# Writing the output over the input image, spreading chunk decays by one selection product, and a reordered head with fourteen extra products

## The chip, the cores and the metric

The kernel runs on one core of one Trainium2 chip. The metric is the device time of the whole program in microseconds (us), the median over several runs.

## The reference, cut to what matters

The input is a batch of 4 images, 128 channels by 32 x 32 pixels in float32, so each image is a 128 x 1024 matrix. Two layers follow each other. The first is an attention block: group norm, q, k, v, a softmax over 1024 x 1024 scores, projection, and the residual. The second is a Mamba-2 block:

```python
u = layernorm(tokens)                       # per token, 128 channels
z, xBC, dt = split(u @ in_w.T)
dt = softplus(dt + dt_bias)                 # 4 heads
x, B, C = split(silu(depthwise_conv4(xBC)))
state = state * exp(dt * A) + (dt * x) outer B   # per token and head
y = state . C + D * x
y = rmsnorm(y * silu(z)) ; out = y @ out_w.T
out = x_in + out * sigmoid(se2(relu(se1(mean(out)))))
```

The recurrence is computed in chunks of 128 tokens. With la = dt * A the log of one token's decay, three things are needed per chunk: the matrix L of decays between all pairs of tokens in it, the decay from the chunk's start to each token (`decay_in`, the exponential of the running sum of la), and the decay over the whole chunk (`chunk_decay`, the exponential of the sum of la over all 128 tokens).

## The kernel before, in words

Each image (a, b, c, d) goes through about 315 named steps. The string `ORDER` (line 59) lists all 1267 steps of the four images in one sequence, and each engine walks that list and issues only the steps that are its own (the loops `for kind, n, b, _ in STEPS`). The order on every engine's queue is therefore the order of that string, written out by hand or by a planner, and every dependence is a semaphore wait in front of an instruction. An instruction that waits holds back everything behind it on its engine. The string also gives, after an `@`, which of the three PSUM banks of the second layer a step fills. The wait for the previous user of that bank to be read is put in by `fill` (line 348 on) from the table `bank_read`.

A half is 512 tokens, four chunks; n = 0 or 1 is the half, and h is one of four heads. `R` = 16 is chunks times heads of a half. Per image and half the steps around the change are:

- `sp0` to `sp8` (DVE, `softplus`): the softplus and la, 16 numbers per token and half. `sp8` writes `la`.
- `dA` (ACT, line 596): exp(la). `dA_rows` (DVE, `rows_split`, lines 671 and 673): the 16 columns in two parts, a rounded one and the rest, 32 columns. `DAT` (PE, line 1051): their transpose, and beside it in the same bank a product of `ones` with la, which is the sum over the chunk. `dA_T` (DVE, line 857): the transposed rows times a mask, `dA_head`, 128 x 512 in the rounded type float32r. `L` (PE, four of them): one product of a row selector with `dA_head`. `l` (DVE, line 872): a scan over each gives L.
- `cd` (ACT, line 603): exp of the chunk sums, `chunk_decay`.
- `Dec` (PE): 16 products in float32, one per chunk and head, each of 32 output partitions by 128 columns, la against the triangular matrix `upto`; every product is two instructions. `decay` (ACT, line 610): exp of the result, `decay_in`. `yo` (DVE, line 901) multiplies by it.
- `y` (DVE, line 907) writes the tile `y`, `g` (POOL, line 484) gates it, `sq`, `Ss`, `ms`, `y_pow`, `y_rows`, `YrT`, `y_T`, `YrB`, `y_b` form the norm, `Out` and `o` (line 926) the output product, `SeA`, `hdn`, `SeB`, `tha`, `att` the squeeze, `XR` (line 1156) a transpose of the residual, and `fin` (line 936) the final sum.

`fin` writes over the tile `y` (`o_img, fin = y, y`), and the SP queue sends it to memory (line 394). So `y` of the next image first waits for that transfer:

```python
wait(dve, yo_dx_ready, b, n + 1)
wait(dve, out_sent[n], b - 1, 16)
```

The head of the program: POOL writes constants, DVE builds the selection masks (`head_of`, `chunk_of`, `head_mask`, lines 657 to 666), then `gn_stats0`, `gn_dev0`, `gn_ve0`, `gn_aff0` (DVE), `gn_mm10` and `gn_mm20` (PE) and `gn_pow0` (POOL) form the group norm of image a. `h_hi` and `h` (ACT, lines 516 and 510) and `h_lo` (DVE, line 776) write the normalised image in two parts, `Q`, `q_hi` (line 522), `q_lo` (line 780) form the query, `S` the scores (three products of 128 x 512 each), `max` (line 784), `exp` (line 533), `T` and `pT` the transposed probabilities, and `PV` the product with the values. `gn_stats1` is the statistics of images b to d: six instructions on DVE. `kq_mm`, `vp_mm`, `win_mm` and `kq_ev`, `vp_ev`, `win_s`, `win_ev` prepare weights. Tiles of PSUM are called `scores`, `turn` (V and T), `attn_out` (PV) and `mamba` (the second layer).

## Time and profile before

| | |
|---|---|
| median of 3 runs | 328.7 us (328.65 to 328.84) |
| the profiled execution | 328.64 us |
| its span, first to last instruction | 326.9 us |
| busy: PE (matmul) / weight load / DVE | 284.5 / 232.1 / 261.0 us |
| busy: ACT / POOL | 187.3 / 81.9 us |
| mean granted TensorE clock | 0.974 of full |

The profiled execution took 1.7 us more than its span. Busy time of an engine does not say that it sets the time: the stretches of the program differ, and the rows below give them separately. A matmul's duration includes the way through the array, so products in a row overlap, and what one costs is the distance from start to start.

### The profile page before, as it was taken

To read this page: it belongs to the slowest core of one execution; us is meant where nothing else is said; L and a number is where in the kernel's file an instruction comes from. 1 tells how busy PE (TensorE), PEld (TensorE's weight loads), DVE (VectorE), ACT (ScalarE), POOL (GpSimd) and SP (SyncE) were. 2 spreads that over 40 slices of the span, in tenths; PEclk is the share of its full clock that TensorE was granted. 3 is DMA by queue.
4 is the path that set the end of the run, shared out by engine and by line. 5 is a ranking of instruction groups with operands and counts; after the bars stand their busy time and mean duration, and the time that the engine had idled before them with its cause. 6 is when DMAs were issued, how large, how long until landed. Compare 5 with 4: busy or idle time off the path is not lost.

```text
span 326.9 us, 6452 instructions
## 1 busy us (share of the span) xinstructions
PE 284.5 (87%) x2206; PEld 232.1 (71%) x2206; DVE 261.0 (80%) x586; ACT 187.3 (57%) x347; POOL 81.9 (25%) x99
## 2 busy tenths in 40 slices
PE   0598999999999999899999999999999988756663
PEld 0477897897879778676787877887987765445542
DVE  4674475997798978969989998988999988996523
ACT  1324577978786855666587656566574835641011
POOL 6000100001011025541502522162023176107340
PEclk9999999999999999999999999999999999996777
DMA  7900000000000000000000000000000010000101
GB/s 216 369 6 1 2 0 3 0 2 0 2 1 3 0 2 2 0 3 1 2 1 9 25 34 1 2 0 3 3 0 2 2 64 1 3 0 2 64 0 66
DMA packets 3791, 7.34 MB, mean 22 GB/s; under 512 B 656, under 2 KB 1584, under 8 KB 3760
## 3 DMA queue, kind: packets, MB, share of 16 engines
q1 hardware_dynamic: 3216, 6.72, 5.7%
q8 instruction: 19, 0.31, 0.4%
q10 hardware_dynamic: 544, 0.21, 0.2%
q14 instruction: 12, 0.10, 0.1%
HBM read 4.83 MB, written 2.10 MB: 21 GB/s over the span
## 4 chain that ended last, share of the span: by engine, by line
PE 57%; DVE 26%; issue 7%; ACT 4%; POOL 2%; DMA 2%; DVEq 1%; ACTq 0%; POOLq 0%
PE mamba L947 20%; PE attn_out L947 12%; PE scores L947 12%; PE turn L1015 6%; DVE L L872 4%; DVE pre L822 3%; DVE neg_max L784 3%; PE turn L947 2%; DMA out<-y 2%; DVE gn_raw L707 1%; PE mamba L1073 1%; DVE scanned L892 1%; DVE L L884 1%; DVE y L936 1%; DVE y L907 1%
## 5 line engine op out<-in xcount | busy, mean ns | idle before, releaser
L947 PE MATMUL attn_out<-values,pT 128*128 128x129 f32 x512 | 66.8, 276 | 0.3 <-DVE res L793 0.2
L947 PEld LDWEIGHTS attn_out<-values,pT 128*128 128x128 f32 x512 | 62.9, 191 | 4.2 <-issue 2.8
L533 ACT ACTIVATE probs<-scores,neg_max 128x512 f32<-128x512 f32 x64 | 42.8, 684 | 25.8 <-DVE neg_max L784 20.4
L784 DVE TENSOR_REDUCE neg_max<-scores 128x1 f32<-128x1024 f32 x32 | 39.0, 1218 | 15.5 <-PE scores L947 15.1
L539 ACT ACTIVATE pT<-turn 128x512 f32<-128x512 f32 x64 | 37.4, 594 | 14.4 <-PE turn L1015 8.9
L872 DVE TENSOR_TENSOR_SCAN L<-mamba,ident 128x512 f32<-128x512 f32 x32 | 38.2, 1212 | 2.3 <-PE mamba L947 2.1
L1015 PE MATMUL turn<-ident,probs 128*128 128x128 f32 x256 | 37.8, 273 | 0.0
L822 DVE SCALAR_TENSOR_TENSOR pre<-raw,vec,pre 128x512 f32<-128x512 f32 x48 | 37.5, 789 | 0.2
L947 PE MATMUL scores<-h_hi,q_hi 128*128 128x512 f32 x64 | 31.4, 491 | 3.4 <-ACT probs L533 2.5
L1015 PEld LDWEIGHTS turn<-ident,probs 128*128 128x128 f32 x256 | 30.2, 141 | 5.8 <-issue 3.3
L445 POOL TENSOR_TENSOR ln_rstd<-ln_var,neg_half 128x4 f32<-128x4 f32 x8 | 8.5, 1066 | 81.1 <-DVE ln_var L804 81.1
L463 POOL TENSOR_TENSOR xend<-xdt,to_end 128x512 f32<-128x512 f32 x8 | 9.8, 1228 | 74.3 <-DVE xdt L865 39.0
L947 PE MATMUL scores<-h_hi,q_lo 128*128 128x512 f32 x64 | 25.8, 404 | 0.0
L947 PE MATMUL mamba<-u,winC 128*128 128x512 f32 x48 | 24.9, 604 | 0.9 <-DVE L L872 0.4
L947 PE MATMUL scores<-h_lo,q_hi 128*128 128x512 f32 x64 | 25.6, 400 | 0.0
L884 DVE TENSOR_TENSOR L<-L,mamba 128x512 f32<-128x512 f32 x32 | 21.3, 678 | 1.0 <-PE mamba L947 1.0
L456 POOL TENSOR_TENSOR gate<-gate,zv 128x512 f32<-128x512 f32 x16 | 20.5, 1286 | 3.6 <-ACT gate L584 3.4
L947 PEld LDWEIGHTS scores<-h_hi,q_hi 128*128 128x128 f32 x64 | 12.3, 192 | 11.1 <-issue 7.6
L947 PE MATMUL mamba<-dA_head,pick_chunk 128*128 128x512 f32 x32 | 14.3, 468 | 2.4 <-ACT BT L616 0.6
L623 ACT ACTIVATE stateT<-scanned 128x512 f32<-128x512 f32 x8 | 9.2, 1145 | 12.1 <-DVE scanned L892 12.1
L484 POOL TENSOR_TENSOR xs<-y,gate 128x512 f32<-128x512 f32 x8 | 11.0, 1380 | 13.8 <-DVE y L907 13.8
L947 PEld LDWEIGHTS scores<-h_hi,q_lo 128*128 128x128 f32 x64 | 12.3, 192 | 2.9
(189 smaller groups left out, 572.1 us busy)
## 6 DMA issues: line engine op xcount, KB each, us to landing
res<-in_x_tok SPq DMA_DIRECT2D x4, 512.0 KB, 8.1
out<-y SPq DMA_DIRECT2D x8, 256.0 KB, 2.0
x_all<-in_x SPq DMA_DIRECT2D x3, 512.0 KB, 8.0
x_all<-in_x SPq DMA_DIRECT2D x2, 256.0 KB, 3.2
winT<-in_in_wT SPq DMA_DIRECT2D x1, 194.0 KB, 6.4
wqkv<-in_qkv_w ACTq DMA_DIRECT2D x1, 192.0 KB, 3.6
wpT<-in_proj_wT SPq DMA_DIRECT2D x1, 64.0 KB, 3.6
ob_row<-in_proj_b SPq DMA_DIRECT2D x1, 64.0 KB, 5.5
```

The costliest lines, as they stand in the source:

```text
L456: pool.tensor_tensor(gate[:, half], gate[:, half], zv[:, half], ALU.add if part else ALU.mult).then_inc(gate_ready.sem, 1)
L463: pool.tensor_tensor(xend[:, rows, :], xdt[:, rows, :], to_end[:, rows].unsqueeze(2).broadcast_to([P, R, HEADDIM]), ALU.mult).then_inc(xen ...
L484: pool.tensor_tensor(y2[:, half], y[:, half], gate[:, half], ALU.mult).then_inc(y2_ready.sem, 1)
L533: act.activation(probs[:, i % 2, half_of(h)], scores[:, half_of(h)], ACT.Exp, bias=neg_max[:, i:i + 1]).then_inc(exp_done.sem, 1)
L539: act.activation(pT[:, i % 2, QUAD * h:QUAD * (h + 1), :], bank[:, :].rearrange("p (a b) -> p a b", a=QUAD), ACT.Copy).then_inc(pT_ready.s ...
L623: act.activation(stateT[:, n, :, :], scanned[:, n, :, :].rearrange("s e c -> s c e"), ACT.Copy).then_inc(stc_ready.sem, 1)
L784: V.tensor_reduce(neg_max[:, n:n + 1], scores[:, :], AX.X, ALU.max, negate=True).then_inc(max_ready.sem, 1)
L822: V.scalar_tensor_tensor(pre[:, k, half_of(n)], raw[:, k, n * HALF + j:(n + 1) * HALF + j], vec[:, at + j:at + j + 1], pre[:, k, half_of(n ...
L872: V.tensor_tensor_scan(L[:, HEADS * n:HEADS * (n + 1), :].rearrange("p a b -> p (a b)"), bank[:, :], ident4[:, :, :].rearrange("p a b -> p ...
L884: V.tensor_tensor(M[:, HEADS * n:HEADS * (n + 1), :], L[:, HEADS * n:HEADS * (n + 1), :], bank[:, tile(c)].unsqueeze(1).broadcast_to([P, H ...
L947: return T.matmul(o, w, v, start=start, stop=stop)
L1015: last = T.transpose(bank[:, tile(c)], probs[:, i % 2, tile(QUAD * h + c)], ident[:, :])
```

## The change

It does four things.

1. `fin` writes into `x_all`, the input image of the same batch, and the SP queue sends from there. `y` waits for `fin` of the image before in place of its transfer.
2. A new step `Cum` (PE) takes a bank of its own and computes from la two sums of 16 columns: the running sum (`upto`) and the chunk's sum (`ones`, until now in `DAT`). A new step `dec` (ACT) takes exp of the running sum. `cd` reads the chunk's sum from that bank. `dA_rows` splits exp(la) and exp(running sum) together, 32 columns, and `DAT` transposes both. The mask keeps the new rows by chunk, and `Dec` is one product of a head selector with `dA_head`, which now comes after `dA_T`. `decay` is a copy in place of an exponential.
3. The masks are built otherwise: four reductions in place of two, `head_sel` of 128 columns and one more copy, and the big mask is a sum of two broadcast tiles in place of a copy.
4. `ORDER` is another order throughout, the head included, with two steps `warm3` and `warm11` on PE: 3 and 11 products of `ident` with itself, 128 x 128 in float32, into `scores`, without a wait.

```diff
 ORDER = """
-gn_stats0 kq_mm gn_mm10 vp_mm gn_dev0 gn_mm20 vp_ev gn_ve0 gn_pow0 gn_aff0 kq_ev h_hi0a win_s h_hi1a win_mm h0a h1a
-h_lo0a xob0a h_lo1a gn_stats1 Q0a V0a@1 q_hi0a q_lo0a gn_mm11 v0a xob1a Q1a S0a q_hi1a alog q_lo1a xob0b S1a V1a@1
-max0a gn_dev1 exp0a v1a S2a exp1a T0a@1 gn_mm21 pT0a S3a T1a@1 max1a PV0a pT1a PV1a exp2a T2a@0 inv0a res0a S4a pT2a
-exp3a S5a T3a@0 max2a PV2a pT3a win_ev PV3a exp4a exp5a T4a@0 S6a gn_ve1 inv1a pT4a gn_pow1 res1a stats0a S7a T5a@0
-max3a PV4a pT5a xob1b PV5a exp6a exp7a T6a@0 inv2a stats1a S8a res2a pT6a xob0c S9a gn_aff1 stats2a T7a@1 max4a PV6a
...
-stc1d XR0c@1 fin0c m5d gate3d Yo1d@1 m6d Y0d@2 yo1d m7d XR1c@1 yo_dx1d y0d Y1d@0 fin1c g0d y1d g1d sq0d Ss0d@0 sq1d
-ms0d Ss1d@2 y_pow0d Out0d@0 ms1d y_rows0d y_pow1d YrT0d@2 y_T0d YrB0d@2 y_rows1d YrT1d@1 y_b0d y_T1d YrB1d@1 o0d
-Out1d@2 y_b1d XR0d@0 o1d SeA0d@2 XR1d@1 hdn0d SeB0d@2 tha0d att0d fin0d fin1d
+gn_stats0 warm3 vp_mm gn_mm10 vp_ev kq_mm gn_dev0 xob0a gn_mm20 kq_ev gn_ve0 gn_pow0 gn_aff0 xob1a h0a wo_s h_hi0a
+win_s h_hi1a h_lo0a h1a warm11 Q0a h_lo1a q_hi0a Q1a q_lo0a q_hi1a S0a q_lo1a gn_stats1 S1a win_mm V0a@1 V1a@0 max0a
+gn_mm11 xob0b exp0a xob1b exp1a S2a v0a gn_dev1 S3a v1a T0a@0 max1a T1a@1 pT0a PV0a exp2a alog exp3a S4a pT1a S5a PV1a
+max2a T2a@0 inv0a T3a@1 xob0c exp4a gn_mm21 exp5a S6a gn_ve1 pT2a xob1c gn_pow1 S7a pT3a res0a T4a@0 max3a PV2a pT4a
+PV3a exp6a exp7a S8a inv1a res1a gn_aff1 T5a@0 stats0a S9a xob0d pT5a h0b T6a@1 stats1a max4a PV4a PV5a win_ev exp8a
+exp9a S10a pT6a xob1d S11a inv2a res2a T7a@0 stats2a max5a T8a@1 pT7a PV6a h1b PV7a exp10a exp11a S12a inv3a pT8a
...
+Yo0d@0 xend1d m1d dx0d U1d@1 yo0d m2d gate2d SeB0c@0 m3d tha0c G1d@0 att0c st1d dx1d yo_dx0d m4d stc1d XR0c@1 gate3d
+m5d fin0c Yo1d@2 m6d Y0d@1 yo1d m7d XR1c@2 yo_dx1d y0d Y1d@0 fin1c g0d y1d g1d sq0d Ss0d@2 sq1d ms0d Ss1d@0 y_pow0d
+y_rows0d ms1d YrT0d@1 y_pow1d Out0d@0 y_T0d YrB0d@2 y_rows1d YrT1d@1 y_b0d y_T1d o0d YrB1d@2 Out1d@1 y_b1d o1d SeA0d@2
+hdn0d SeB0d@2 XR0d@1 tha0d XR1d@0 att0d fin0d fin1d
 """.split()
...
 PREPARE = ("gn_stats", "gn_mm1", "gn_dev", "gn_mm2", "gn_ve", "gn_pow", "gn_aff", "kq_mm", "kq_ev", "vp_mm", "vp_ev",
-           "win_s", "wo_s", "win_mm", "win_ev", "alog")
+           "win_s", "wo_s", "win_mm", "win_ev", "alog", "warm")
 ATTENTION = {"xob", "h", "h_hi", "h_lo", "Q", "q_hi", "q_lo", "V", "v", "S", "max", "exp", "T", "pT", "PV", "inv", "res"}
...
         pick_row = sb("pick_row", [P, QUAD], F32R)
-        head_of = sb("head_of", [P, HEADS])
-        chunk_of = sb("chunk_of", [P, QUAD])
+        head_sel = sb("head_sel", [P, HEADS, HEADDIM], F32R)
+        row_head, row_chunk = sb("row_head", [P, 2, HEADS]), sb("row_chunk", [P, 2, QUAD])
         head_mask = sb("head_mask", [P, HEADS, P])
...
         la = sb("la", [P, 2, R])
-        dA = sb("dA", [P, 2, R])
+        dA = sb("dA", [P, 2, 2 * R])
         dA_rows = sb("dA_rows", [P, 2, P])
...
         y = sb("y", [P, TOKENS])
-        o_img, fin = y, y
+        o_img = y
         y2 = xs
...
         filled = {kind: signal(f"{kind}_filled", n) for kind, n in (
-            ("V", 2), ("T", 16), ("UT", 2), ("InX", 2), ("InBC", 2), ("InZ", 2), ("Dt", 2), ("DAT", 2), ("Dec", 2),
+            ("V", 2), ("T", 16), ("UT", 2), ("InX", 2), ("InBC", 2), ("InZ", 2), ("Dt", 2), ("Cum", 2), ("DAT", 2), ("Dec", 2),
             ("L", 8), ("XsT", 2), ("BT", 2), ("G", 2), ("U", 2), ("Yo", 2), ("Y", 2), ("Ss", 2), ("YrT", 2),
...
         sp_step = signal("sp_step", 2 * SP_STEPS)
+        dec_ready = signal("dec_ready", 2)
         dA_ready, dA_rows_step, dA_T_ready = signal("dA_ready", 2), signal("dA_rows_step", 4), signal("dA_T_ready", 2)
...
                      "InBC": [(raw_ready["bc"], 1)], "InZ": [(zt_ready, 1), (zv_ready, 1)], "Dt": [(dtx_step, 1)],
-                     "DAT": [(dA_T_ready, 1), (cd_ready, 1)], "Dec": [(decay_ready, 1)], "L": [(l_ready, 1)],
+                     "Cum": [(dec_ready, 1), (cd_ready, 1)], "DAT": [(dA_T_ready, 1)], "Dec": [(decay_ready, 1)], "L": [(l_ready, 1)],
                      "XsT": [(xdt_ready, 1)], "BT": [(BT_ready, 1)], "G": [(M_ready, 4)], "U": [(st_ready, 1)],
...
                     wait(sp, fin_ready, b, n + 1)
-                    sp.dma_start(out_d[b][:, half_of(n)], fin[:, half_of(n)]).then_inc(out_sent[n].sem, 16)
+                    sp.dma_start(out_d[b][:, half_of(n)], x_all[:, b * TOKENS + n * HALF:b * TOKENS + (n + 1) * HALF]
+                                 ).then_inc(out_sent[n].sem, 16)
             for n in range(2):
...
                     wait(act, sp_step, b, SP_STEPS * (n + 1))
-                    act.activation(dA[:, n, :], la[:, n, :], ACT.Exp, scale=1.0 / A_SCALE).then_inc(dA_ready.sem, 1)
+                    wait(act, dA_rows_step, b - 1, 2 * n + 2)
+                    act.activation(dA[:, n, 0:R], la[:, n, :], ACT.Exp, scale=1.0 / A_SCALE).then_inc(dA_ready.sem, 1)
+                elif kind == "dec":
+                    wait(act, dA_rows_step, b - 1, 2 * n + 2)
+                    bank = take(act, b, "Cum", n)
+                    act.activation(dA[:, n, R:2 * R], bank[:, 0:R], ACT.Exp, scale=1.0 / A_SCALE).then_inc(dec_ready.sem, 1)
                 elif kind == "cd":
                     wait(act, st_ready, b - 1, n + 1)
-                    wait(act, dA_T_ready, b, n + 1)
-                    bank = take(act, b, "DAT", n)
+                    bank = take(act, b, "Cum", n)
                     chunks = slice(1, QUAD) if n == 0 else slice(0, QUAD - 1)
                     act.activation(chunk_decay[:, n, :, :, 1:QUAD],
-                                   bank[:, P:P + R].rearrange("s (c h) -> s h c", h=HEADS)[:, :, chunks]
+                                   bank[:, R:2 * R].rearrange("s (c h) -> s h c", h=HEADS)[:, :, chunks]
                                    .unsqueeze(2).broadcast_to([P, HEADS, HEADDIM, QUAD - 1]),
...
                     bank = take(act, b, "Dec", n)
-                    act.activation(decay_in[:, half], bank[:, :], ACT.Exp, scale=1.0 / A_SCALE
-                                   ).then_inc(decay_ready.sem, 1)
+                    act.activation(decay_in[:, half], bank[:, :], ACT.Copy).then_inc(decay_ready.sem, 1)
                 elif kind == "bt":
...
             V.tensor_scalar(center[:, :], ident[:, :], 1.0 / P, None, ALU.subtract)
-            V.tensor_reduce(head_of[:, :], ident[:, 0:2 * R].rearrange("r (q h) -> r h q", h=HEADS), AX.X, ALU.add)
-            V.tensor_reduce(chunk_of[:, :],
-                            ident[:, 0:2 * R].rearrange("r (s c h) -> r c s h", s=2, c=QUAD), AX.XY, ALU.add)
-            V.memset(head_mask[:, :, 0:1], 0.0)
+            rows = ident[:, 0:4 * R].rearrange("r (s k c h) -> r k s c h", s=2, k=2, c=QUAD)
+            for k in range(2):
+                V.tensor_reduce(row_head[:, k, :], rows[:, k].rearrange("r s c h -> r h s c"), AX.XY, ALU.add)
+                V.tensor_reduce(row_chunk[:, k, :], rows[:, k].rearrange("r s c h -> r c s h"), AX.XY, ALU.add)
             step_done(V.tensor_tensor(pick_row[:, :], ident[:, 0:QUAD], ident[:, QUAD:2 * QUAD], ALU.add))
-            V.tensor_copy(pick_chunk[:, :], chunk_of[:, :])
-            step_done(V.tensor_copy(head_mask[:, :, 1:P], head_of[:, :].unsqueeze(2).broadcast_to([P, HEADS, P - 1])))
+            V.tensor_copy(pick_chunk[:, :], row_chunk[:, 0, :])
+            V.tensor_copy(head_sel[:, :, :], row_head[:, 1, :].unsqueeze(2).broadcast_to([P, HEADS, HEADDIM]))
+            V.tensor_copy(head_mask[:, :, 0], row_chunk[:, 1, :])
+            step_done(V.tensor_tensor(head_mask[:, :, 1:P], row_head[:, 0, :].unsqueeze(2).broadcast_to([P, HEADS, P - 1]),
+                                      row_chunk[:, 1, :].unsqueeze(2).broadcast_to([P, HEADS, P - 1]), ALU.add))
             def rows_split(rows, value, signal, b, n):
...
                     if k == SP_STEPS - 1:
-                        wait(dve, filled["Dec"], b - 1, n + 1)
-                        wait(dve, filled["DAT"], b - 1, n + 1)
+                        wait(dve, filled["Cum"], b - 1, n + 1)
+                        wait(dve, dA_ready, b - 1, n + 1)
                     softplus(b, n, k).then_inc(sp_step.sem, 1)
...
                     wait(dve, dA_ready, b, n + 1)
+                    wait(dve, dec_ready, b, n + 1)
                     wait(dve, filled["DAT"], b - 1, n + 1)
...
                     wait(dve, filled["L"], b - 1, QUAD * (n + 1))
+                    wait(dve, filled["Dec"], b - 1, n + 1)
                     bank = take(dve, b, "DAT", n)
...
                     wait(dve, yo_dx_ready, b, n + 1)
-                    wait(dve, out_sent[n], b - 1, 16)
+                    wait(dve, fin_ready, b - 1, n + 1)
                     bank = take(dve, b, "Y", n)
...
                     bank = take(dve, b, "XR", n)
-                    V.scalar_tensor_tensor(fin[:, half], o_img[:, half], att[:, :], bank[:, :], ALU.mult, ALU.add
-                                           ).then_inc(fin_ready.sem, 1)
+                    V.scalar_tensor_tensor(x_all[:, b * TOKENS + n * HALF:b * TOKENS + (n + 1) * HALF], o_img[:, half],
+                                           att[:, :], bank[:, :], ALU.mult, ALU.add).then_inc(fin_ready.sem, 1)
             for kind, n, b, _ in STEPS:
...
                 b0, b1 = (0, 1) if n == 0 else (1, BATCH)
-                if kind == "gn_mm1":
+                if kind == "warm":
+                    for _ in range(n):
+                        mm(scores[:, 0:P], ident[:, :], ident[:, :])
+                elif kind == "gn_mm1":
                     pe.wait_ge(gn_stats_done.sem, n + 1)
...
                     bank, done = fill(pe, b, "DAT", n)
-                    T.transpose(bank[:, 0:P], dA_rows[:, n, :], ident[:, :])
-                    mm(bank[:, P:P + R], ones[:, :], la[:, n, :]).then_inc(done, 1)
+                    T.transpose(bank[:, 0:P], dA_rows[:, n, :], ident[:, :]).then_inc(done, 1)
+                elif kind == "Cum":
+                    wait(pe, sp_step, b, SP_STEPS * (n + 1))
+                    bank, done = fill(pe, b, "Cum", n)
+                    mm(bank[:, 0:R], upto[:, :], la[:, n, :])
+                    mm(bank[:, R:2 * R], ones[:, :], la[:, n, :]).then_inc(done, 1)
                 elif kind == "Dec":
-                    wait(pe, sp_step, b, SP_STEPS * (n + 1))
+                    wait(pe, dA_T_ready, b, n + 1)
                     bank, done = fill(pe, b, "Dec", n)
-                    for c in range(QUAD):
-                        for h in range(HEADS):
-                            r = HEADS * c + h
-                            last = mm(bank[h * HEADDIM:(h + 1) * HEADDIM, tile(c)],
-                                      la[:, n, r:r + 1].broadcast_to([P, HEADDIM]), upto[:, :])
-                    last.then_inc(done, 1)
+                    mm(bank[:, :], head_sel[:, :, :].rearrange("r h d -> r (h d)"),
+                       dA_head[:, n, :, :].rearrange("r h i -> r (h i)")).then_inc(done, 1)
                 elif kind == "L":
...
```

## Rows read from the trace of the kernel before

**Rows 1.** The page: busy time of each engine.
```profile
PE 284.5 (87%) x2206; PEld 232.1 (71%) x2206; DVE 261.0 (80%) x586; ACT 187.3 (57%) x347; POOL 81.9 (25%) x99
```

**Rows 2.** The chain of waits, shares of the span by engine.
```profile
PE 57%; DVE 26%; issue 7%; ACT 4%; POOL 2%; DMA 2%; DVEq 1%; ACTq 0%; POOLq 0%
```

**Rows 3.** Busy time by stretch: five engines, then granted clock and DMA.
```profile
53.00:250.00 197.00, 190.85 (x1513) 159.18 (x1512) 175.76 (x384) 135.50 (x254) 46.90 (x43) 1.00 0.01 4
250.00:293.00 43.00, 34.99 (x338) 25.02 (x337) 39.43 (x84) 24.34 (x47) 15.12 (x13) 1.00 0.04 13
...
293.00:303.00 10.00, 5.74 (x27) 4.74 (x26) 7.34 (x13) 1.16 (x1) 6.15 (x7) 0.66 0.01 2
303.00:313.00 10.00, 6.33 (x84) 5.03 (x84) 4.45 (x8) 1.23 (x2) 4.31 (x4) 0.83 0.14 52
313.00:327.00 14.00, 7.67 (x36) 4.93 (x36) 4.22 (x14) 1.74 (x5) 1.54 (x2) 0.76 0.11 39
```

**Rows 4.** The head in order of time: start, duration, engine, line (idle before, releaser).
```profile
7.31 0.42 DVE L666 COPY head_mask<-head_of 128x508 f32<-128x508 f32 x1
...
13.03 1.52 ACT L516 ACTIVATE h_hi<-x_all,gn_bias,gn_scale 128x512 fp32r<-128x512 f32 x2 [8.27 <-DVE gn_bias L728]
...
17.10 3.65 DVE L707 BATCH_NORM_STATS2 gn_raw<-x_all 128x6 f32<-128x512 f32 x6
...
17.19 0.77 PE L947 MATMUL scores<-h_hi,key_query_hi 128*128 128x512 f32 x1
...
18.62 1.91 PE L947 MATMUL turn<-value_proj,h 128*128 128x128 f32 x8
18.86 0.69 ACT L522 ACTIVATE q_hi<-scores,col 128x512 fp32r<-128x512 f32 x1 [2.90 <-PE scores L947]
...
21.05 0.70 DVE L780 SCALAR_TENSOR_TENSOR q_lo<-scores,col,q_hi 128x512 fp32r<-128x512 f32 x1
...
26.58 1.23 DVE L784 TENSOR_REDUCE neg_max<-scores 128x1 f32<-128x1024 f32 x1 [1.20 <-PE scores L947]
...
28.98 0.40 PE L947 MATMUL scores<-h_lo,q_hi 128*128 128x512 f32 x1
...
29.21 0.40 PE L947 MATMUL scores<-h_hi,q_lo 128*128 128x512 f32 x1
```

**Rows 5.** PE in order of time around one `Dec`.
```profile
70.56 1.08 PE L947 MATMUL mamba<-upto,la 128*32 128x128 f32 x32
71.57 0.50 PE L947 MATMUL mamba<-dA_head,pick_chunk 128*128 128x512 f32 x1
71.91 1.05 PE L947 MATMUL turn<-value_proj,h 128*128 128x128 f32 x8
```

**Rows 6.** Groups by line and shape: busy us, mean ns of one, idle before.
```profile
L947 PE MATMUL mamba<-la,ones 128*128 128x16 f32 x16 | 2.3, 222 | 0.0
...
L596 ACT ACTIVATE dA<-la 128x16 f32<-128x16 f32 x8 | 1.7, 212 | 3.7 <-DVE la L699 3.7
```

**Rows 7.** Groups of DVE from 262 to 311 us.
```profile
L884 DVE TENSOR_TENSOR L<-L,mamba 128x512 f32<-128x512 f32 x8 | 5.3, 677 | 0.0
...
L907 DVE TENSOR_TENSOR y<-mamba,th 128x512 f32<-128x512 f32 x4 | 2.8, 692 | 3.6 <-DMA out<-y 3.0 <-PE mamba L947 0.6
```

**Rows 8.** The end in order of time.
```profile
307.12 1.08 PE L947 MATMUL mamba<-L,xdt 128*32 128x128 f32 x32
307.38 0.74 DVE L936 SCALAR_TENSOR_TENSOR y<-y,att,mamba 128x512 f32<-128x512 f32 x1
...
310.27 0.69 DVE L907 TENSOR_TENSOR y<-mamba,th 128x512 f32<-128x512 f32 x1 [2.15 <-DMA out<-y]
...
311.10 1.13 PE L947 MATMUL mamba<-ones,sq 128*128 128x128 f32 x8 [2.90 <-DVE y L907]
...
314.69 1.91 PE L947 MATMUL mamba<-xs,woutT 128*128 128x512 f32 x2
...
316.39 0.42 PE L1131 MATMUL mamba<-ident,y_rows 128*128 128x128 f32 x1
```

121 lines of the change are left out of this document (60 added, 61 removed).

## The prediction

> **What bounds the kernel now.** I read the busy times first [rows 1]: PE 284.5 us of the span of 326.9 us, DVE 261.0. An average over the span decides nothing, so next the chain of waits [rows 2]: PE holds 57% of it and DVE 26%, which says two engines take turns. The busy time by stretch says where [rows 3]. From 53 to 250 us PE is busy 190.85 of 197 us, 97%, and DVE 89%: PE's queue sets the pace, and what it no longer has to do can come off. From 250 to 293 us the attention of the last image runs out, and DVE is the fuller one, 39.43 of 43. From 293 us on neither is full (PE 21 us of 34 and at a granted clock of 0.66 to 0.83, DVE 16): there the program waits along one chain, and only a shorter chain counts. The head is also a chain, up to the first `max0a` at 26.58 us [rows 4]. So there are four stretches and four sums.
>
> **The head.** Added: DVE builds the masks before `gn_stats0`, and the big mask copy ends at 7.73 us just ahead of it [rows 4]. Two reductions more, two more copies, and a sum of 508 columns where a copy of 0.42 us stood. A sum of 512 columns of the same kind takes 0.68 us [rows 7], so that is 0.26, and small steps follow each other at 0.1 to 0.2 us each: 0.8 in all. On DVE `vp_ev`, `xob0a` and `kq_ev` now stand ahead of `gn_ve0`, while `vp_mm` and `kq_mm` surround `gn_mm10` on PE. Part of them fills waits, and I charge 0.6. Thus `h` starts at 13.03 + 1.4 = 14.4 in place of 13.03.
> Removed: PE had `win_mm` between `h_hi` and `Q0a`, which began at 17.19, 4.2 after the start of `h_hi`. In the new order `h0a`, `h_hi0a` (0.76 each) and `h_lo0a` (0.7) lead to `Q0a` at 16.7. The larger part is `gn_stats1`: 3.65 us on DVE from 17.10 [rows 4], ahead of `q_lo0a`, whose input was ready at 19.55 and which started at 21.05; and `Q1a` stood on PE behind `gn_mm11`, which needs these statistics. Now `gn_stats1` comes after `q_lo1a`, and `win_mm` and both `V` after `S1a`. From `Q0a` at 16.7 through `q_hi`, `q_lo` (0.7 to 0.75 each) and `S0a` I get `q_lo1a` done at 20.5, and `S1a` at 21.4. Next late is DVE itself: `gn_stats1` and three aggregates, 3.9 us, stand before `max0a`, so 24.4. `win_mm` and `V` lie beside it on PE. That is 26.58 - 24.4 = 2.2 us gained.
> The fourteen products: eight products of 128 x 128 last 1.91 us in the head and 1.05 us at 71.91 [rows 4, 5], the three of `S` start 0.23 us apart once the pace is up (28.98, 29.21) [rows 4]. So PE ran at its half level, 1.2 GHz, in the head, and the rise came late. `warm11` issues after `gn_mm20` at about 12 us, where PE would wait, and lasts at the half pace 22 instructions of 1.91 / 8 = 0.24 us or less, some 5 us: up to `Q0a` at 16.7, hence nearly free. If PE is at 2.4 GHz by then, the 2.2 holds. If not, `Q0a` to `S1a` cost some 0.7 more on the chain and `win_mm` and `V` do not fit behind DVE. The price of the warm products themselves is 0 to 0.5 us; I take 0.
> The Trainium skill ("TensorE: Matmul & The Clock Gate", Part 1) says that the array is throttled by default, that activity releases it and idleness takes it back, with a phase that differs from run to run. By that rule the gain could differ between executions, and the pause of PE after `V1a` could take it back; the sum of this head would then be 0 in place of -2.2. The sum goes by the rows' pace.
>
> **`Dec`, `Cum`, `dec`.** A `Dec` begins at 70.56 and the next product at 71.57: 1.01 us of PE, eight times [rows 5]. The new one is one product like the three of `S`, 0.23 us apart [rows 4]. The chunk's product moves from `DAT` to `Cum`; a second like it is new, two instructions of 222 ns that overlap [rows 6]: 0.2 us. So 1.01 - 0.23 - 0.2 = 0.58 per half, 4.6 in all. Seven of the eight stand before the last `PV15d`, where PE's queue sets the pace: 4.1. How much comes off: all of it if nothing else is late, none if waits take it back. The three banks now serve 24 `Cum`, `DAT`, `Dec` in place of 16, and each turn must be read first. I take two thirds, -2.7, because PE had 3% idle and DVE 11% there [rows 3].
> The Trainium skill ("Perfetto Trace Analysis", Identifying the Most-Contended Engine) holds that matmul occupancy is a poor measure and the share of weight loads a better one. Here weight loads fill 159.18 of 197 us, 81%, in that stretch [rows 3]. By that rule PE has a fifth of slack and the saving would come out nearer a third, -1.4.
> ACT gets eight `dec` of 0.21 us, like `dA` [rows 6], 1.7 us beside 69% occupancy: nothing. `decay` costs the same as a copy. DVE's `dA_rows` grow from 16 to 32 columns: 0 to 0.03 us each for 16 instructions, and I take 0.2 into the head's round number.
> The wait: `dA_rows` (DVE) now also waits for `Cum` (0.3 with its way through the array) and `dec` (0.21 and two signals), about 0.7 us more from la to the rows. Behind it on DVE stand `max` and `inv` of attention. The order puts one to eight other DVE steps between `sp8` and `dA_rows` in each of the eight halves, never less than a scan or two products with the chunk matrix, 1.2 us [rows 7], so I cost it at nothing; without cover it is 0.7 x 8 = 5.6 us.
>
> **After the attention.** DVE is the fuller engine here. The new order leaves more behind `PV15d`: `m6c`, `m7c`, `dA_rows0d`, `dA_T0d` for one tap of a convolution, `conv_bc3d`. `m` takes 0.68 [rows 7], `dA_T` and the tap are 512-column steps too and cancel, and the two small ones of `dA_rows` take some 0.2 us: 2 x 0.68 + 0.2 = +1.6 us. The waits of `y` on transfers were 3.0 us over three times [rows 7], of which 2.15 at 310.27 [rows 8] and 0.85 in this stretch: -0.85. The last `Dec` left the chain ahead of `xdt0d`: about -0.6. Sum +0.2.
>
> **The end.** `fin1c` ends at 308.12 and `Y1d` at 308.20; `y1d` starts at 310.27 only because of the transfer [rows 8]. Now it starts at 308.25: -2.0. What is late next is `Y1d`, in the same place. The first `Ss` waited until 311.10 because it shared a bank with `Y1d` [rows 8]; it has another bank now and starts at about 309.6. In the old order `Out0d`, 1.91 us at the half clock, ran from 314.69 ahead of the first transpose of the norm at 316.39 [rows 8], whose rows were ready a microsecond earlier. The new order has it behind. -1.0 for both. Sum -3.0; with the clock lower or higher in between, -2 to -3.5.
>
> **Sum.** -2.2 - 2.7 + 0.2 - 3.0 = -7.7 against the profiled execution's 328.64 us (span 326.9 and 1.7 around it), 0.06 under the median of 328.7. That gives 321.0 us. A measurement of this kernel can tell 0.2% or 0.66 us from no change.
>
> **The rivals.** (1) *The middle gives back.* Everything between 53 and 290 us stands in another order, and the three banks turn over 8 times more. For it: DVE at 89 to 92% leaves little room. Against: the sums of work per image are otherwise the same. Then the Dec saving is 0 and the new order costs 2: -2.2 + 2 + 0.2 - 3.0 = -3.0, 325.7 us. (2) *The head's clock stays low*, or the statistics before `max0a` come no sooner: the head gives 0, -5.5, 323.2 us. (3) *The decay chain becomes the bound, slower.* `dA_rows` blocks DVE while PE and ACT, each in order, come to `Cum` and `dec` behind attention products and exponentials. Ahead of `Cum` on PE can stand as much as a `V`, 1.05 us [rows 5], ahead of `dec` on ACT a 512-column step like `q_hi`, 0.69 us [rows 4]. At 1.0 us per half the 8 halves give back the whole 7.7; at 1.2 us it is 9.6, giving 330.6 us. It decides from 1.0 us of mean stall. Against: the 1.2 us and more of DVE work between `sp8` and `dA_rows`. (4) *The order is better than its parts*: the new interleaving also takes half of the 6 us that PE is idle from 53 to 250 us [rows 3]: -7.7 - 3.1 = -10.8, 317.8 us.
>
> **Numbers.** Forecast 0.50, rival 1 0.20, rival 2 0.12, rival 3 0.08, rival 4 0.10. The range from 317.0 to 327.0 holds rival 4, the forecast, rivals 2 and 1. It leaves out rival 3 and the ends. Faster by over 0.2%: 0.90, with a little of rival 1 going to the same, 0.03; slower 0.07.
>
> **What would show it.** `max0a` near 24.4 us, and the products of `Q0a` 0.23 us apart and not 0.43. No `mamba<-upto,la` group of 256 instructions, PE busy some 5 us less apart from the warm ones. No wait of line 907 on a transfer. From `y1d` to the end 1 us shorter. The last `PV15d` about 5 us earlier. The forecast is wrong if DVE waits for ACT before `dA_rows` by 1 us or more, if PE's idle time from 53 to 250 us grows from 6 us by as much as was saved, or if the stretch after `PV15d` is longer by more than 2 us.

## The result and the profile after

| | before | after |
|---|---|---|
| median, 4 runs of each side by side | 328.8 us (328.65 to 329.86) | 317.05 us (316.62 to 317.42) |
| the profiled execution | 328.64 us | 316.84 us |
| its span | 326.9 us | 315.0 us |
| mean granted TensorE clock | 0.974 | 0.984 |

The ratio is 0.9636, with a 95% interval of 0.9611 to 0.9661. The change takes 11.7 us off where 7.7 was forecast. The median lies 0.05 us above the lower end of the range, 317.0; the ratio times 328.8 us gives 316.8, just below it. The page's busy times and the granted clock in 40 slices, to hold against [rows 1] and [rows 2]:

```profile
PE 280.2 (89%) x2002; PEld 228.1 (72%) x2002; DVE 260.7 (83%) x589; ACT 187.1 (59%) x355; POOL 79.7 (25%) x99
PEclk9999999999999999999999999999999999969997
```

DVE and ACT have the work they had (260.7 us against 261.0, 187.1 against 187.3). The page's shares of the chain add up to 17% only, since here it could be followed back over the last part alone, so they can't be read beside [rows 2]. The windows can. After, by stretch, columns as in [rows 3]:

```profile
53.00:240.00 187.00, 180.14 (x1296) 149.00 (x1294) 166.61 (x363) 128.97 (x247) 42.93 (x41) 1.00 0.01 4
...
281.00:291.00 10.00, 8.00 (x40) 5.38 (x41) 9.23 (x13) 4.64 (x9) 1.34 (x2) 0.82 0.01 2
291.00:301.00 10.00, 7.39 (x102) 5.89 (x100) 9.54 (x16) 1.67 (x3) 8.30 (x10) 1.00 0.09 35
```

In the middle PE is as full as before (96% against 97%). The change of character is late: in the two stretches of 10 us DVE is now busy 9.23 and 9.54 us, where [rows 3] had 7.34 and 4.45, and the granted clock is 0.82 and 1.00 in place of 0.66 and 0.83.

**Four marks.** Four instructions can be found in every trace: the first `max0a`, the last product of the last `PV15d` on PE, the last `inv` on DVE (`inv7d`), and the last `y` (`y1d`). They cut the span in five stretches:

| stretch | before | after | difference | forecast by the same cut |
|---|---|---|---|---|
| start to `max0a` | 26.58 | 24.22 | -2.4 | -2.2 |
| `max0a` to the last `PV15d` (263.0; 257.7) | 236.4 | 233.5 | -2.9 | -2.7 |
| `PV15d` to `inv7d` (263.45; 259.57) | 0.45 | 1.87 | +1.4 | +1.6 |
| `inv7d` to `y1d` (310.27; 300.04) | 46.82 | 40.47 | -6.35 | -0.85 - 0.6 - 2.0 = -3.45 |
| `y1d` to the end | 16.63 | 14.96 | -1.7 | -1.0 |
| sum | 326.9 | 315.0 | -11.9 | -7.7 |

The prediction's "After the attention" began where PE ends `PV15d`. Most of the DVE steps that its +1.6 compares (`m7c`, `dA_T0d`, `conv_bc3d`) run ahead of `inv7d`, so it stands in the third line, and the waits and the last `Dec` in the fourth. That the third line agrees says little: `y0c` (0.69 us) stood behind `inv7d` before and stands ahead of it now, and the forecast did not have that. The cut that does not depend on the place of `inv7d` is from the last `PV15d` to `y1d`, before and after:

```profile
263.00:310.27 47.27, 33.89 (x303) 23.83 (x301) 37.90 (x77) 18.04 (x34) 21.11 (x19) 0.89 0.06 23
257.70:300.04 42.34, 32.97 (x252) 22.31 (x251) 38.32 (x80) 19.18 (x37) 18.78 (x18) 0.92 0.04 14
```

It is 4.9 us shorter where 1.85 was forecast (+1.6 - 3.45), and this is where the sum failed. DVE's work in it grew by 0.4 us, 37.9 to 38.3, and its idle time fell from 9.4 to 4.0. The windows of the kernel before, `inv7d` to `y1d` and then to the end:

```profile
263.50:310.30 46.80, 33.39 (x296) 23.45 (x288) 37.42 (x77) 18.04 (x34) 20.63 (x19) 0.89 0.06 20
310.30:326.90 16.60, 8.80 (x44) 5.90 (x44) 5.04 (x16) 2.34 (x5) 3.30 (x3) 0.80 0.09 33
```

The same two of the changed kernel:

```profile
259.60:300.00 40.40, 31.69 (x244) 21.32 (x243) 36.41 (x76) 18.07 (x35) 18.34 (x18) 0.92 0.04 14
300.00:315.00 15.00, 7.42 (x44) 5.20 (x44) 5.14 (x16) 2.97 (x6) 4.02 (x4) 0.89 0.14 52
```

DVE does 37.4 us of work before and 36.4 after, and its idle time is 46.8 - 37.4 = 9.4 us before and 40.4 - 36.4 = 4.0 after: the idle time that went lies all in here, and it is 5.4 of the 6.35 us. The view of its waits names them. Before, in this stretch (total us, times, longest):

```profile
DVE y L907 <- DMA out<-y: 3.0, 3, 2.2
DVE scanned L892 <- PE mamba L947: 1.8, 1, 1.8
DVE th L901 <- PE mamba L947: 0.9, 1, 0.9
DVE xdt L865 <- PE mamba L1073: 0.8, 2, 0.5
DVE dtx L808 <- PE mamba L947: 0.7, 1, 0.7
DVE y L907 <- PE mamba L947: 0.6, 1, 0.6
```

After:

```profile
DVE y_T L933 <- PE mamba L1149: 1.1, 2, 0.7
DVE xs L850 <- PE mamba L960: 0.6, 1, 0.6
DVE L L884 <- PE mamba L960: 0.5, 2, 0.3
DVE th L913 <- PE mamba L960: 0.4, 1, 0.4
```

The transfers' 3.0 us are gone. Of the five waits of 0.6 to 1.8 us for PE, 4.8 in all, three are gone and two are down to 0.4 and 0.2, while others have come, the largest 1.1. The net of these is 9.4 - 4.0 - 3.0 = 2.4 us. The forecast had counted the transfers and 0.6 for the last `Dec`. The last 1.0 of the 6.35 is work (37.4 to 36.4) that now stands ahead of `inv7d`, `y0c` among it.

### The profile page after: what moved, and what is told of

Its sections match the earlier page's. It is cut to its first block and busy times, and to the rows that moved or that the text cites. A ratio compares the mean times of both kernels' runs of the same rounds, so it can differ in the third digit from the quotient of the medians.

```text
span 315.0 us, 6079 instructions
## 1 busy us (share of the span) xinstructions
PE 280.2 (89%) x2002; PEld 228.1 (72%) x2002; DVE 260.7 (83%) x589; ACT 187.1 (59%) x355; POOL 79.7 (25%) x99
## 5 line engine op out<-in xcount | busy, mean ns | idle before, releaser
L542 ACT ACTIVATE pT<-turn 128x512 f32<-128x512 f32 x64 | 37.9, 595 | 19.5 <-PE turn L1032 15.3
L833 DVE SCALAR_TENSOR_TENSOR pre<-raw,vec,pre 128x512 f32<-128x512 f32 x48 | 36.0, 761 | 0.2
L960 PE MATMUL scores<-h_hi,q_hi 128*128 128x512 f32 x64 | 29.1, 454 | 3.4 <-ACT probs L536 2.6
L459 POOL TENSOR_TENSOR gate<-gate,zv 128x512 f32<-128x512 f32 x16 | 20.5, 1279 | 3.1 <-ACT zv L592 2.9
L960 PE MATMUL mamba<-dA_head,pick_chunk 128*128 128x512 f32 x32 | 15.6, 497 | 1.7 <-DVE L L884 0.9
L491 POOL TENSOR_TENSOR y_rstd<-ms,neg_half 128x4 f32<-128x4 f32 x8 | 8.7, 1082 | 25.4 <-DVE ms L922 25.3
L560 ACT ACTIVATE raw<-mamba,col 128x512 f32<-128x512 f32 x16 | 11.0, 688 | 5.6 <-PE mamba L960 5.5
```

Of the source, the lines that this page charges most:

```text
L459: pool.tensor_tensor(gate[:, half], gate[:, half], zv[:, half], ALU.add if part else ALU.mult).then_inc(gate_ready.sem, 1)
L491: pool.tensor_tensor(y_rstd[:, four], ms[:, four], neg_half[:, four], ALU.pow).then_inc(y_rstd_ready.sem, 1)
L542: act.activation(pT[:, i % 2, QUAD * h:QUAD * (h + 1), :], bank[:, :].rearrange("p (a b) -> p a b", a=QUAD), ACT.Copy).then_inc(pT_ready.s ...
L560: act.activation(raw[:, k, PAD + n * HALF:PAD + (n + 1) * HALF], bank[:, :], ACT.Identity, bias=col[:, bias:bias + 1]).then_inc(raw_ready[ ...
L833: V.scalar_tensor_tensor(pre[:, k, half_of(n)], raw[:, k, n * HALF + j:(n + 1) * HALF + j], vec[:, at + j:at + j + 1], pre[:, k, half_of(n ...
L960: return T.matmul(o, w, v, start=start, stop=stop)
```

## The experiments

Twelve kernels. A "2 x 2" of orders comes first, because the order was the part that the prediction had not costed. For all of them: the median, and the ratio to the kernel before on the same chip with its interval. Spans and marks are of each one's profiled execution. The kernels ran on several chips, on which the kernel before had medians of 329.25 to 330.46 us. So a difference between two of them is taken here from their ratios, times 328.8 us, and by the intervals it is good to 1.2 to 1.7 us.

### The new code in the old order

The order before, with `Cum`, `dA`, `dec` and `cd` at the place of `dA`, with `Dec` and `decay` behind `dA_T` where they stood ahead of it, no products of `ident`, and the bank of one of the old steps changed:

```diff
-... dA0a ... DAT0a@0 ... dA_T0a ... cd0a ...
+... Cum0a@0 dA0a dec0a cd0a ... DAT0a@0 ... dA_T0a ...
```

> The code of the changed kernel (output over the image, Cum, dec, the rounded product, the new masks) in the order of the kernel before, with Cum, dec and cd at the place of dA and Dec behind dA_T; no warm products. It has every part but the order. Theory A (the new order after the attention and in the head is worth about 6 to 7 us of the 11.7): 322 to 324 us. Theory B (the parts bring it, the order little beyond the head's 2.4 us): 318 to 320 us. If the old order does not suit the new chain (dA_rows waits for Cum and dec on DVE): 325 us or more.

Measured: 338.1 us, ratio 1.0251 (1.0219 to 1.0284). So the same code is 8.3 us slower than before in nearly the old order, and 12.0 faster in the new one. In the profiled execution, 8.9 us longer in span, `inv7d` comes at 269.35, 5.9 later than before, `inv7d` to `y1d` is 4.7 longer, and the end 1.7 shorter. A part of the 5.9 shows in two groups of the whole program, `dA_rows` and `upto` of this kernel:

```profile
L682 DVE CAST dA_rows<-dA 128x32 fp32r<-128x32 f32 x8 | 1.4, 178 | 4.7 <-ACT dA L605 3.5 <-issue 1.1
...
L960 PE MATMUL mamba<-la,upto 128*128 128x16 f32 x16 | 2.8, 250 | 3.3 <-DVE la L710 2.1 <-DVE L L896 1.1
```

and of the changed kernel:

```profile
L682 DVE CAST dA_rows<-dA 128x32 fp32r<-128x32 f32 x8 | 1.4, 178 | 0.1
...
L960 PE MATMUL mamba<-la,upto 128*128 128x16 f32 x16 | 2.9, 256 | 0.3 <-DVE la L710 0.2
```

In the old order DVE sits idle 4.7 us before `dA_rows`, waiting for `dec`: this is rival 3, at the place it named. In the kernel before it was 1.1 us, one wait for `dA`, and in the new order it is 0.1. The cover of this wait is made by the order. The 4.7 come in three waits, the longest 2.5 us, where the prediction gave 5.6 as 0.7 in each of eight halves; that the two sums are near each other is chance. These waits lie before the last `PV15d` and can't be the 4.7 us of the ending too. There, at a granted clock of 0.70, DVE waits for PE before `scanned` (3.8 us) and `xdt` (3.4), where the kernel before had 1.8 and 0.8.

### The new order up to `PV15d`, then the old one

The order after up to and with `PV15d`, then the rest of the steps in the order of the kernel above, with four banks changed:

```diff
-... PV15d m6c dec0d dA0d cd0d dA_rows0d stc1c m7c DAT0d@1 y0c Yo1c@0 dA_T0d g0c inv7d ...
+... PV15d m6c m7c dA0d dec0d cd0d dA_rows0d DAT0d@0 dA_T0d stc1c Dec0d@0 Yo1c@1 decay0d yo1c yo_dx1c inv7d ...
```

> The changed kernel up to PV15d of the last image; what is then left stands in the order of the kernel before (with Cum, dec and Dec at the places of the kernel with the old order). Up to 259.6 us it must run like the changed kernel. Theory A (the order behind the attention keeps DVE and PE filled, and that is the 6.4 us between the last PV and y1d that no term of the forecast had): the stretch from the last PV to y1d takes 45 to 47 us and not 40.5, so 5 to 7 us slower than the changed kernel, about 322 to 324. Theory B (the parts, the missing waits on transfers above all, shortened it): at most 2 us slower.

Measured: 330.0 us (328.0 to 332.8), ratio 1.0013 (0.9981 to 1.0045). In the new code the order of the steps behind `PV15d` alone is worth 12.4 us, as much as the whole gain. The profiled execution was the longest of its twelve, 332.79. In it the last `PV15d` to `inv7d` takes 5.3 us (1.8 in the changed kernel) and `inv7d` to `y1d` 51.9, at a granted clock of 0.71.

### The old order first, then the new one behind `PV15d`

The steps behind `PV15d` in the order after, at the end, and all others in the order of the first experiment; three steps stand earlier for a bank's sake, and six banks are changed:

```diff
-... PV15d yo1c conv_bc3d Y0c@0 yo_dx1c inv7d ...
+... PV15d conv_bc3d Y0c@0 gate3c m6c dec0d dA0d cd0d dA_rows0d stc1c m7c DAT0d@1 y0c Yo1c@0 dA_T0d g0c inv7d ...
```

> The mirror: the order of the kernel before up to the last PV, and behind it the steps of the changed kernel's ending in its order. The run with the old order had its last PV 5.9 us later than the kernel before; this one has the same start. Theory A: from there the ending takes 40 to 42 us to y1d as in the changed kernel and 15 more, so 324 to 328 us. Theory B (an ending is only as good as what stands before it): 331 to 338 us.

Measured: 329.9 us, ratio 1.0034 (0.9994 to 1.0073). The ending is good here too, 41.9 us from `inv7d` to `y1d` (40.5 after), but `max0a` to `inv7d` takes 244.6 us in place of 235.4. The waits for `dA_rows` are the same three as in the first experiment.

So, with the new code throughout, the ratios are 1.0251 (old start, old ending), 1.0013 (new, old), 1.0034 (old, new) and 0.9636 (new, new). The new start alone is worth 7.8 us, the new ending alone 7.1, both together 20.2. The 5.3 over the sum, good to some 2 us, can't be given to either.

### The ending in the old order, with products in the idle time of PE

The order of "The new order up to `PV15d`", with 67 products of `ident` with itself in the ending:

```diff
-... raw_x1d sp17d conv_bc5d Cum1d@1 ... dA_T1d Dec1d@2 decay1d XsT0d@2 ... BT1d@0 ... fin0c ... Ss0d@0 sq1d ms0d Ss1d@2
+... raw_x1d sp17d conv_bc5d warm5 Cum1d@1 ... dA_T1d warm6 Dec1d@2 decay1d warm5 XsT0d@2 ... warm8 BT1d@0 ...
```

> The changed kernel with the old order behind the last PV (which took 51.9 us to y1d at a granted clock of 0.71, against 40.5 us at 0.92) and 67 such products in its idle stretches. It splits the 11.4 us between order and clock. Theory A (the clock is most of it): 43 to 46 us to y1d, 321 to 325 us in all. Theory B (the order is most of it): 49 us or more to y1d, 328 us or more.

Measured: 324.4 us, ratio 0.9867 (0.9832 to 0.9903), 4.8 us faster than without them. One stretch without the products:

```profile
290.00:303.00 13.00, 8.96 (x39) 7.08 (x38) 9.81 (x15) 4.01 (x8) 0.49 (x1) 0.63 0.01 1
```

The same with them:

```profile
290.00:303.00 13.00, 12.43 (x108) 12.07 (x108) 11.31 (x18) 3.07 (x4) 6.15 (x7) 1.00 0.01 1
```

The granted clock is 1.00 in place of 0.63, and DVE gets 11.31 us of work done in place of 9.81. Thus of the 12.4 us that the old ending costs in the new code, 4.8 go through TensorE's clock: waits of DVE leave PE idle, the clock falls, and the products that DVE waits for are late. The other 7.6 are the order itself.

### The same idle-time products in the new ending

```diff
-u_tok1d L1d@2 l1d g1c decay0d UT1d@0 ... YrT1c@1 ... DAT1d@1 ... XsT0d@1 ... Dec1d@1 ...
+u_tok1d L1d@2 l1d g1c decay0d warm6 UT1d@0 ... warm4 YrT1c@1 ... warm5 DAT1d@1 ... warm2 XsT0d@1 ... warm7 Dec1d@1 ...
-... Ss0d@2 ... YrB1d@2 ... SeA0d@2
+... warm10 Ss0d@2 ... warm3 YrB1d@2 ... warm6 SeA0d@2
```

> The changed kernel with 53 such products in twelve idle stretches of its ending. Its clock is 0.62 from 277 to 286 us and 0.89 behind y1d. Theory A: 1 to 2 us faster than the changed kernel, 315 to 316 us, which would beat both. Theory B: the same or slower.

Measured: 317.3 us, ratio 0.9642 (0.9615 to 0.9669): the same as the changed kernel. Its windows, `inv7d` to `y1d` and to the end:

```profile
259.40:299.30 39.90, 36.70 (x314) 28.37 (x313) 36.54 (x76) 18.08 (x35) 18.40 (x18) 1.00 0.04 15
299.30:315.20 15.90, 11.03 (x82) 9.31 (x81) 5.13 (x16) 2.97 (x6) 4.00 (x4) 0.93 0.13 51
```

The clock rises from 0.92 to 1.00 and the first stretch gets 0.6 us shorter; the second is 0.9 longer, which the extra products in it would explain if they stand in the chain. A last kernel therefore left out those behind `y1d`:

```diff
-... warm10 Ss0d@2 ... warm3 YrB1d@2 ... warm6 SeA0d@2
+... Ss0d@2 ... YrB1d@2 ... SeA0d@2
```

> The changed kernel with only the 34 idle-time products that stand ahead of y1d of the last image; the 19 behind it, which made the last stretch 0.9 us longer, are left out. In the run with all 53 y1d came 0.7 us earlier. Theory A: that stays and the last stretch is 15.0 us again, 0.7 us faster than the changed kernel, about 316.3 us. Theory B: PE is at half clock behind y1d again by another phase and nothing is left, 317 us.

Measured: 317.2 us, ratio 0.9632 (0.9591 to 0.9672). `inv7d` to `y1d` is 39.9 us and the rest 15.6, at a granted clock of 0.83: nothing kept, and the products behind `y1d` were not all of the 0.9. At the same clock of 1.00, the old ending takes 48.8 us from the last `PV15d` to `y1d` (the experiment above, where 4.2 of them lie ahead of `inv7d`) and the new one 41.8: in the new code the order is worth 7.1 there, near the 7.6 of the ratios.

### The same in the kernel before

```diff
-... stc0d l5d c1d l6d BT1d@0 ... XsT1d@0 ... G1d@0 ... XR0c@1 ... Yo1d@1 ... Ss0d@0 ... Ss1d@2
+... stc0d l5d c1d l6d warm8 BT1d@0 ... warm4 XsT1d@0 ... warm6 G1d@0 ... warm10 XR0c@1 ... warm6 Yo1d@1 ... warm20 Ss0d@0 ...
```

> The kernel before with 59 products of ident with itself put into seven idle stretches of PE behind BT1d of the last image, each a little shorter than the idle time there at full rate; all else as before. Theory A (in the ending PE's half clock turns DVE's waits longer, and that is a good part of what the ending cost): the granted clock from 290 us on goes from 0.66 to 0.83 up to near 1, and the program is 2 to 4 us faster. Theory B (the ending is bound by the order of its steps, the clock follows): within 1 us, or slower because the products delay what is behind them.

Measured: 326.1 us, ratio 0.9884 (0.9852 to 0.9916), 3.8 us by the ratio. The two profiled executions are only 2.1 us of span apart, and 0.7 of that is at `max0a`, ahead of anything that was changed. `inv7d` to `y1d` went from 46.8 to 46.3, at 0.96 against 0.89, and the end from 16.6 to 16.0. But the profiled execution of this kernel, 326.58, was among the longer of its six (two took 324.3), and that of the kernel before, 328.64, among the shorter (328.5 to 330.6 beside this one). So what the low clock cost in the kernel before lies between the half microsecond of these two traces up to `y1d` and the 3.8 of the ratio, and stays open.

### The output over `y` again

```diff
-                    sp.dma_start(out_d[b][:, half_of(n)], x_all[:, b * TOKENS + n * HALF:b * TOKENS + (n + 1) * HALF]
-                                 ).then_inc(out_sent[n].sem, 16)
+                    sp.dma_start(out_d[b][:, half_of(n)], y[:, half_of(n)]).then_inc(out_sent[n].sem, 16)
...
-                    wait(dve, fin_ready, b - 1, n + 1)
+                    wait(dve, out_sent[n], b - 1, 16)
...
-                    V.scalar_tensor_tensor(x_all[:, b * TOKENS + n * HALF:b * TOKENS + (n + 1) * HALF], o_img[:, half],
+                    V.scalar_tensor_tensor(y[:, half], o_img[:, half],
```

> The changed kernel with the output written over the tile y again, and y waiting for the transfer of the image before; all else as changed. Theory A (the interleaving of the last image filled the stretch after the attention; the transfer was only a wait at the end): y1d stands about 1 us behind fin1c in this order, so a transfer of 2.0 us and its signal delay it by 1.9 us; the waits of c cost up to 0.9 more: 1.5 to 3 us slower than the changed kernel. Theory B (the waits of y on transfers held DVE back through the whole stretch from 262 us on, and taking them away is most of what was gained there): 4 to 6 us slower.

Measured: 325.9 us, ratio 0.9879 (0.9847 to 0.9911), 8.0 us slower than the changed kernel (8.5 of span), for waits of

```profile
DVE y L918 <- DMA out<-y: 4.2, 3, 2.3
```

on transfers. The stretches behind the first of these waits show a part of the rest. With the output over `y`:

```profile
268.00:277.00 9.00, 8.17 (x28) 4.86 (x26) 5.33 (x20) 4.98 (x10) 1.11 (x1) 0.71 0.01 2
277.00:286.00 9.00, 5.92 (x25) 3.52 (x24) 8.70 (x16) 4.13 (x9) 2.71 (x2) 0.86 0.01 2
286.00:295.00 9.00, 7.31 (x38) 5.27 (x37) 7.96 (x12) 3.88 (x7) 0.32 (x1) 0.76 0.00 0
```

The same stretches in the changed kernel:

```profile
268.00:277.00 9.00, 7.05 (x36) 4.34 (x35) 7.17 (x27) 5.77 (x12) 1.11 (x1) 1.00 0.00 2
277.00:286.00 9.00, 6.51 (x22) 3.46 (x22) 8.15 (x14) 3.88 (x7) 2.72 (x2) 0.62 0.01 2
286.00:295.00 9.00, 6.58 (x45) 5.48 (x45) 8.84 (x14) 2.63 (x6) 4.42 (x6) 1.00 0.00 0
```

Behind the first wait the clock is 0.71 where it was 1.00, and DVE does 5.33 us of work in the 9 where it did 7.17. The changed kernel has its low stretch too, 0.62, a little later. Over the 27 us it is 0.78 against 0.87, and 22.0 us of DVE's work against 24.2. Behind `y1d` the clock is 0.72 and the end takes 16.8 us in place of 15.0.

### The output over the input image in the kernel before

```diff
-                    sp.dma_start(out_d[b][:, half_of(n)], fin[:, half_of(n)]).then_inc(out_sent[n].sem, 16)
+                    sp.dma_start(out_d[b][:, half_of(n)], x_all[:, b * TOKENS + n * HALF:b * TOKENS + (n + 1) * HALF]
+                                 ).then_inc(out_sent[n].sem, 16)
...
-                    wait(dve, out_sent[n], b - 1, 16)
+                    wait(dve, fin_ready, b - 1, n + 1)
...
-                    V.scalar_tensor_tensor(fin[:, half], ...
+                    V.scalar_tensor_tensor(x_all[:, b * TOKENS + n * HALF:b * TOKENS + (n + 1) * HALF], ...
```

> The kernel before with only the output written over the input image. Forecast's terms: y1d no longer waits 2.15 us, and y0c and y1c not 0.4 each: 2 to 3 us faster. Theory B (a stall of DVE there also lowers PE's clock, so it costs more than its length): 4 to 7 us faster, with PE's clock in the last 35 us nearer to 1.

Measured: 325.3 us, ratio 0.9895 (0.9847 to 0.9942). In the profile it is 3.7 us of span: 2.2 up to `y1d` (44.6 against 46.8) and 1.5 behind it. The steps behind `y1d` stand in their old order and old banks here. Its end in order of time:

```profile
308.14 0.69 DVE L908 TENSOR_TENSOR y<-mamba,th 128x512 f32<-128x512 f32 x1 [0.28 <-PE mamba L948]
...
310.96 1.16 PE L948 MATMUL mamba<-ones,sq 128*128 128x128 f32 x8 [0.50 <-ACT sq L628]
...
311.96 1.02 PE L948 MATMUL mamba<-xs,woutT 128*128 128x512 f32 x2
...
312.82 0.27 PE L1132 MATMUL mamba<-ident,y_rows 128*128 128x128 f32 x1
```

and the end of the changed kernel:

```profile
300.04 0.69 DVE L919 TENSOR_TENSOR y<-mamba,th 128x512 f32<-128x512 f32 x1
...
302.86 1.16 PE L960 MATMUL mamba<-ones,sq 128*128 128x128 f32 x8 [0.27 <-ACT sq L634]
...
304.34 0.33 PE L1149 MATMUL mamba<-ident,y_rows 128*128 128x128 f32 x1 [0.32 <-DVE y_rows L684]
304.51 1.09 PE L960 MATMUL mamba<-xs,woutT 128*128 128x512 f32 x2
```

From `y1d` to the first transpose of the norm it is 316.39 - 310.27 = 6.12 us before [rows 8], 4.68 here and 4.30 after. `Out0d` ahead of it costs 0.4 when it lasts 1.02 us; before it lasted 1.91. The second `Ss` was long there too:

```profile
313.08 1.81 PE L947 MATMUL mamba<-ones,sq 128*128 128x128 f32 x8 [0.85 <-ACT sq L627]
```

It lasts 1.16 us here, from the same point (2.8 us behind the start of `y1d` in all three). And `Ss0d` starts 1.17 us behind the start of `y1d`, where `sq` releases it, so another bank would gain it nothing.

### The new head in the kernel before

The order up to `exp3a` as after, the rest of the steps as before; masks and `Dec` as before:

```diff
-gn_stats0 kq_mm gn_mm10 vp_mm gn_dev0 gn_mm20 vp_ev ...
+gn_stats0 warm3 vp_mm gn_mm10 vp_ev kq_mm ... warm11 Q0a h_lo1a q_hi0a Q1a q_lo0a q_hi1a S0a q_lo1a gn_stats1 S1a win_mm ...
```

> The kernel before with the changed kernel's order up to exp3a only, warm products included, old masks; behind it the old order. max0a should come at about 23.6 us in place of 26.58. Theory A (PE's queue sets the pace from there on and carries the gain to the end): 2 to 3.5 us faster than the kernel before. Theory B (DVE or a later wait takes it back before the last PV): less than 1 us.

Measured: 327.5 us, ratio 0.9933 (0.9902 to 0.9964). `max0a` comes at 23.55, 3.0 us earlier, and `inv7d` still 2.7 earlier. By the ratio that is 2.2 us, in the profiled execution 1.3 of span. There `inv7d` to `y1d` takes 49.3 us in place of 46.8, at a granted clock of 0.83 against 0.89, and 0.3 is left at `y1d`. What the head gains arrives nearly whole at the end of the attention and is mostly lost in an ending that stalls. The same fourteen products last 5.0 us here, and the first three of `Q0a` behind them start at 15.91, 16.49 and 16.91, still at the half level; 0.23 us apart they are only from 17.54 on.

### Without the fourteen products

```diff
-gn_stats0 warm3 vp_mm ... h_lo0a h1a warm11 Q0a h_lo1a q_hi0a
+gn_stats0 vp_mm ... h_lo0a h1a Q0a h_lo1a q_hi0a
```

> The changed kernel without its fourteen products of ident with itself. Theory A (they raise the clock): Q0a to S1a and the six of win and the sixteen of V run at half pace in the head, the products of Q0a 0.43 us apart and not 0.23, and max0a comes 0.7 to 1.5 us later, S2a up to 3 us later: 1 to 3 us slower in all. Theory B (the clock rises in the head anyway, or DVE's statistics hide it): within 0.5 us.

Measured: 318.6 us, ratio 0.9663 (0.9638 to 0.9688), 0.9 us slower than with them, which by the intervals is not clear of noise; in the profiled executions it is 1.2 of span. `Q0a` without the products:

```profile
16.54 0.76 PE L960 MATMUL scores<-h_hi,key_query_hi 128*128 128x512 f32 x1 [4.53 <-DVE h_lo L787]
17.10 0.63 PE L960 MATMUL scores<-h_lo,key_query_hi 128*128 128x512 f32 x1
17.53 0.63 PE L960 MATMUL scores<-h_hi,key_query_lo 128*128 128x512 f32 x1
```

With them, the products of `ident` in the first row:

```profile
11.89 4.11 PE L960 MATMUL scores<-ident 128*128 128x128 f32 x22
...
16.56 0.47 PE L960 MATMUL scores<-h_hi,key_query_hi 128*128 128x512 f32 x1 [0.56 <-DVE h_lo L787]
16.87 0.39 PE L960 MATMUL scores<-h_lo,key_query_hi 128*128 128x512 f32 x1
17.10 0.40 PE L960 MATMUL scores<-h_hi,key_query_lo 128*128 128x512 f32 x1
```

0.43 us from one product to the next is the half level, 0.23 the full one. `max0a` is 0.65 later without, `inv7d` 1.5 and `y1d` 1.2.

### `Dec` as 16 products in its new place

```diff
-                    mm(bank[:, :], head_sel[:, :, :].rearrange("r h d -> r (h d)"),
-                       dA_head[:, n, :, :].rearrange("r h i -> r (h i)")).then_inc(done, 1)
+                    for c in range(QUAD):
+                        for h in range(HEADS):
+                            r = HEADS * c + h
+                            last = mm(bank[h * HEADDIM:(h + 1) * HEADDIM, tile(c)],
+                                      la[:, n, r:r + 1].broadcast_to([P, HEADDIM]), upto[:, :])
+                    last.then_inc(done, 1)
```

with `decay` an exponential again, and `sp8` waiting for `Dec`.

> The changed kernel with the sixteen products per half (each 128 x 32 by 128, from la) in the place of the one rounded product, and the exponential in place of the copy; Cum, dec and the 32 columns stay. PE gets 1.01 - 0.23 = 0.78 us more in each of eight halves, 6.2 us. Theory A (PE's queue sets the pace up to the end of the attention, two thirds of its work show): 3.5 to 5 us slower. Theory B (PE's occupancy overstates, a third shows): 1.5 to 2.5 us slower.

Measured: 322.2 us, ratio 0.9786 (0.9753 to 0.982), 4.9 us slower than the changed kernel (5.1 of span). The eight cost 8 x (1.01 - 0.23) = 6.2 us of PE. In the new order `Dec0d` has moved behind the attention; in the changed kernel it is

```profile
263.66 0.40 PE L960 MATMUL mamba<-dA_head,head_sel 128*128 128x512 f32 x1
```

so six stand before the last `PV15d` (4.7), and they show as 3.2 us at `inv7d`; 1.4 more come up to `y1d`, where the other two are, and 0.5 behind it.

## Why the prediction was right in its sign and too small in its size

**The head: right.** -2.4 against -2.2. `Q0a` starts at 16.56 (16.7), `gn_stats1` at 20.27, just behind the last `q_lo` (20.5), and `max0a` at 24.22 (24.4), with the products 0.23 us apart. Rival 2 fell: the products of `Q0a` ran at the full level, and without the fourteen they did not, and `inv7d` came 1.5 us later.

**`Dec`, `Cum`, `dec`: right.** -2.9 against -2.7 up to the last `PV15d`, which came 5.3 us earlier ("about 5"). The share of PE time that shows was put at two thirds; the experiment on it gives 3.2 of 4.7 us, 69%, up to `inv7d`. The rule of the Trainium skill ("Perfetto Trace Analysis", Identifying the Most-Contended Engine), read as a third, would have given 1.6 there: in a stretch with weight loads at 81% PE's queue did set the pace. How the 2.9 divide between the saving and the order of the middle was not separated.

**The wait of `dA_rows`: right.** Costed at nothing with cover and at 5.6 us without: 0.1 us of idle time in the new order, 4.7 in the old one. Rival 3 is what happens to this code where the order is not made for it. The order was not a detail beside the change, it was the condition under which the code pays.

**After the attention: the step that failed.** The prediction wrote "Sum +0.2" for this part and -2.0 for `y1d` at the end: 1.6 - 0.85 - 0.6 - 2.0 = -1.85 from the last `PV15d` to `y1d`. Measured -4.9. Two terms of it were wrong, and both missed the same way.

The waits, -3.45: DVE's idle time fell by 5.4, so 1.9 more. The prediction took off the waits that an edit removed by name (transfers 3.0, `Dec` 0.6) and left every other wait as the trace of before had it, though its own windows showed DVE at 7.34 and 4.45 of 10 us there [rows 3]. What went besides are waits of DVE for PE.

The work behind `PV15d`, +1.6: it grew by 0.4, so 1.2 less. `m6c` and `dA_rows0d` stand behind `PV15d` in the string, but on DVE's queue `m6c` was done at 257.5 and `dA_rows0d` began at 257.45, ahead of the last product of `PV15d` at 257.7: some 0.9 of it by the prediction's own prices. The order of the string is the order on each engine and not between them.

The transfers did not bring more than forecast: in the kernel before, the output over the input image shortened `inv7d` to `y1d` by 2.2 us, where 2.85 had been taken for it. The other 2.7 of the 4.9 are the order and the new `Dec` together, for which the forecast had +1.0. How they divide was not tried: the 7.1 us between the endings at the full clock are a difference within the new code, whose old ending takes 48.8 us where the kernel before with its output moved takes 45.1. Rival 4 had this mechanism but in the wrong stretch: it took idle time of PE from 53 to 250 us, and that hardly moved (PE is idle 6.9 of 187 us there, before 6.2 of 197). That its 317.8 us lie near the result is luck. One reading was wrong without weight: from 293 us on PE was busy 19.7 us of 34 [rows 3] and not 21.

**The end: the size nearly, the reason not.** -1.7 against -1.0. The prediction gave it to another bank for `Ss0d` and to `Out0d` behind `YrT0d`. The kernel before with only its output moved keeps the old bank and the old order and already has 15.1 us from `y1d` to the end, against 16.6 before and 15.0 after. What shortened it was that PE had not stood still for 2.9 us ahead of `Ss0d`: the second `Ss` lasts 1.16 us and not 1.81, `Out0d` 1.02 and not 1.91. Place and bank are worth 0.4 at most; in the first two experiments, with the new code in the old ending, the end takes 14.9 and 15.0 us.

**The rule on the clock.** The Trainium skill ("TensorE: Matmul & The Clock Gate", Part 1) says that idleness takes the clock back. In the head it could have taken the gain, and the trace has the products at the full pace. It bore on the ending, where the prediction did not use it: with the output over `y` in the new order 4.2 us of waits of DVE cost 8.0, at a granted clock of 0.86 in place of 0.92 from `inv7d` to `y1d` and 0.72 in place of 0.89 behind it. How much of the other 3.8 is the clock was not separated.

**Of the signs that it named:** no `upto,la` group of 256 instructions, no wait of `y` on a transfer, `y1d` to the end over 1 us shorter, all seen. PE's busy time fell by 4.3 us, and the `ident` products added 5.8, so it is 10 less apart from them and not 5; a part of the surplus is products in the ending that ran at the full level.

**Open.** Why the two halves of the order together gain 5.3 us more than one by one, what the low clock cost in the kernel before, and whether an old order with more steps between `Cum` and `dA_rows` would do as well as the new one, which was not tried. No kernel here was clearly faster than the changed one.

## What to carry to other kernels

When a change comes with a new order, read the idle time of the fuller engine in every stretch where none is full: the order can reach it, and the waits that an edit removes by name are only the part that is easy to see. What runs ahead of what has to be read on each engine's own queue. Price a wait of another engine in such a stretch at its length or more: 3.0 us of waits cost 3.5 in the old order and 4.2 cost 8.0 in the new one. And try new code in an order made for it: the same code was 8 us slower than the kernel before in the old order and 12 faster in the new one.

## What the runs showed of the hardware

Behind the 2.9 us in which PE stood still ahead of `Ss0d`, the kernel before ran its first `Ss` still in 1.13 us, and then the second `Ss` and `Out0d` at the half level: 1.81 and 1.91 us. Where PE stood still 1.33 us at that place, with the output over the input image, they took 1.16 and 1.02. The granted clock does not show the half level everywhere. The window of the head without the fourteen products:

```profile
7.00:24.90 17.90, 11.25 (x42) 8.52 (x43) 13.74 (x46) 4.30 (x6) 0.56 (x1) 1.00 0.51 199
```

Its granted clock is 1.00, while the products of `Q0a` follow each other at 0.43 us. There only the distance from start to start tells. A full clock is worth little by itself: in an ending whose waits are few, 53 idle-time products raised it from 0.92 to 1.00 and the time stayed at 317 us; in the new code's old ending, whose waits are many, 67 gave 4.8.
